# Attention scores in fp32 with two halves of the queries beside each other, and projections ahead of the loop

## The reference

```python
def _L1_gnn_ref(x, adj, node_embeddings, Wq, bq, Wk, bk, Wv):
    Q = x @ Wq + bq
    K = x @ Wk + bk
    V = x @ Wv
    score = jnp.einsum('bnc,bmc->bnm', Q, K)
    score = jax.nn.softmax(score, axis=1)
    score = jnp.einsum('bnm,mc->bnc', score, adj)
    out = jnp.einsum('bnm,bmc->bnc', score, V)
    return jax.nn.relu(out)
...
x = _layernorm(x + _L1_gnn_ref(x, adj, ...), axis=-1)
```

## Time and profile before

| | us |
|---|---|
| median of 3 runs | 790.41 (790.21 to 796.23) |
| the profiled execution | 792.9 |
| its span, first to last instruction | 790.8 |
| TensorE (PE) busy | 684.2 |
| VectorE (DVE) busy | 430.1 |
| ScalarE (ACT) busy | 340.7 |
| GpSimd (POOL) busy | 290.8 |

### The profile page before, as it was taken

The page is one execution under the profiler, slowest core; times in us unless marked ns, Lnnn a source line. Parts: engine busy times, 40 slices in busy tenths (PEclk is TensorE's granted clock), DMA queues, the critical chain, the costliest instruction groups (busy, mean ns, idle before and its releaser), DMA issues. The chain is left out here.

```text
span 790.8 us, 9801 instructions
## 1 busy us (share of the span) xinstructions
PE 684.2 (87%) x3408; PEld 474.6 (60%) x3408; DVE 430.1 (54%) x963; ACT 340.7 (43%) x649; POOL 290.8 (37%) x273
## 2 busy tenths in 40 slices
PE   6869988898898896988889847997999999999992
PEld 2767765566567682333233325886776767678882
DVE  1675747667289404656567655111566656671165
ACT  1851334444473504554645521312344646364214
POOL 0350115655448200101041483001567676750036
PEclk9988999999997998999999967999999999999996
DMA  8110030000000120303030010000000000000013
GB/s 307 54 54 2 1 107 0 1 1 1 1 2 0 24 58 1 80 2 79 1 80 1 1 57 1 1 1 0 2 1 1 1 1 0 1 2 1 1 28 80
DMA packets 14931, 20.44 MB, mean 26 GB/s; under 512 B 10064, under 2 KB 10064, under 8 KB 14880
## 3 DMA queue, kind: packets, MB, share of 16 engines
q1 hardware_dynamic: 14368, 18.16, 8.3%
q10 hardware_dynamic: 512, 1.60, 0.6%
HBM read 11.37 MB, written 2.10 MB: 17 GB/s over the span
## 5 line engine op out<-in xcount | busy, mean ns | idle before, releaser
L1879 DVE SCALAR_TENSOR_TENSOR arena<-PS,WT,arena 128x256 f32<-128x256 f32 x160 | 77.4, 484 | 67.2 <-PE PS L2003 43.1
L1551 DVE TENSOR_REDUCE arena<-PS 128x1 f32<-128x1024 f32 x64 | 75.4, 1220 | 44.2 <-PE PS L1249 44.2
L163 POOL TENSOR_TENSOR LN_Y<-LN_V,CN 128x16 f32<-128x16 f32 (+1 forms) x17 | 48.4, 2848 | 71.5 <-DVE LN_V L155 71.5
L1434 POOL TENSOR_TENSOR arena<-arena 128x128 f32<-128x128 f32 x32 | 13.0, 405 | 166.7 <-DVE arena L1557 166.7
L1795 ACT ACTIVATE spare<-PS,WT 128x256 f32<-128x256 f32 x96 | 38.9, 473 | 71.9 <-DVE arena L1879 70.3
L1395 ACT ACTIVATE arena<-PS,arena 128x1024 f32<-128x1024 f32 x44 | 48.7, 1111 | 48.7 <-DVE arena L1551 48.7
L1990 PE MATMUL PS<-WH,KH 128*128 128x512 f32 x128 | 54.3, 424 | 10.5 <-POOL KL L1701 10.0
L1243 PE MATMUL PS<-QMV,KST 128*128 128x512 f32 x128 | 44.7, 440 | 11.5 <-DVE arena L1534 5.3
L1990 PE MATMUL PS<-WH,KL 128*128 128x512 f32 x128 | 51.4, 401 | 0.0
L1990 PE MATMUL PS<-WL,KH 128*128 128x512 f32 x128 | 51.0, 398 | 0.0
L1243 PEld LDWEIGHTS PS<-QMV,KST 128*128 128x128 f32 x128 | 19.6, 188 | 45.0 <-issue 18.2
(11 more groups left out here) (285 smaller groups left out, 1620.1 us busy)
## 6 DMA issues: line engine op xcount, KB each, us to landing
arena<-in_adj_tr SPq DMA_DIRECT2D x8, 512.0 KB, 5.8
arena<-in_x_tr SPq DMA_DIRECT2D x4, 512.0 KB, 8.5
arena<-in_x_nat SPq DMA_DIRECT2D x1, 2048.0 KB, 8.8
KLO<-QMV SPq DMA_DIRECT2D x8, 256.0 KB, 3.4
QMV<-KST SPq DMA_DIRECT2D x8, 256.0 KB, 2.8
KST<-KST SPq DMA_DIRECT2D x8, 256.0 KB, 2.9
out<-arena SPq DMA_DIRECT2D x8, 256.0 KB, 3.4
arena<-in_w SPq DMA_DIRECT2D x2, 512.0 KB, 4.1
```

The lines of the kernel that those rows point to most:

```text
L163: pool.tensor_tensor(LN_Y[:, at:at + n], LN_V[:, at:at + n], CN[:, C_NEGH:C_NEGH + n], ALU.pow).then_inc(ln_rstd, 1)
L1551: dve.tensor_reduce(NMX[:, i, par:par + 1], banks("S", 2 * i + par), AX.XY, ALU.max, negate=True).then_inc(max_ready, 1)
L1879: dve.scalar_tensor_tensor(acc, PS[:, four_banks(t, j), d * F:(d + 1) * F], WT[:, e:e + 1], acc, ALU.mult, ALU.add).then_inc(acc_step, 1)
```

## The change

K and Q are kept in fp32 and not split. `project` uses one order of weights (K above Q) for both graphs of a pair; ScalarE evicts the even graph and VectorE the odd one, with bias, to KQ. DMAs bring the first 512 queries to the low half of the partitions and the last 512 to the high half (MOVED), and then put K into both halves of KQ. A score matmul has 64 rows; the two halves of one graph's queries lie beside each other in the array. Each graph's scores are signalled on their own.

All projections come before the loop: those of pairs 1 to 3 behind adjacency tiles 0 to 2, in banks 0 to 3. The adjacency tiles 6 and 7 move behind the scores of step 0, into banks 6 and 7. The residual stands ahead of the maxima of m = 4. Tensors are laid out anew.

```diff
-        KST = [[rounded(f"KST{i}{par}", at * SLOT + par * N, [P, N]) for par in range(2)] for i, at in enumerate((4, 0))]
-        QMV = [[rounded(f"QMV{i}{par}", at * SLOT + (2 * (1 - i) + par) * N, [P, N]) for par in range(2)] for i, at in enumerate((4, 2))]
-        KLO = [rounded(f"KLO{i}", 2 * SLOT + (2 + i) * N, [P, N]) for i in range(2)]
+        KQ = [[column(4, 0), column(4, 1)], [column(4, 3), spare[:, 0:N]], [column(0, 0), column(0, 1)], [column(0, 2), column(2, 3)]]
+        MOVED = [column(4, 2), spare[:, N:2 * N], column(2, 2), column(0, 3)]
...
-            if i % NT == 2 and i // NT + 1 < BP:
-                fills += [("KQ", 2 * (i // NT + 1)), ("KQ", 2 * (i // NT + 1) + 1)]
...
+        def av_bank(t):
+            return (6 if t >= NT - 2 else 4) + t % 2
...
+                low, high = slice(0, 64), slice(64, 128)
+                for q in range(BP):
+                    for par, evicted in enumerate((k_out, q_out)):
+                        b, both, halves = 2 * q + par, KQ[q][par], MOVED[q][:, par * HALF:(par + 1) * HALF]
+                        sp.wait_ge(evicted, q + 1)
+                        sp.dma_start(halves[low, :], both[high, 0:HALF]).then_inc(q_moved[b], 16)
+                        sp.dma_start(halves[high, :], both[high, HALF:N]).then_inc(q_moved[b], 16)
+                    for par in range(2):
+                        b, both = 2 * q + par, KQ[q][par]
+                        sp.wait_ge(q_moved[b], 32)
+                        sp.dma_start(both[high, :], both[low, :]).then_inc(k_moved[b], 16)
...
+                for t in range(NT - 2):
+                    adjacency_times_values(t)
+                    if t + 1 < BP:
+                        project(t + 1)
 
                 def scores(i):
                     q, m = i // NT, i % NT
-                    if m == 0:
-                        for par in range(2):
-                            pe.wait_ge(khi_moved[par], 16 * (q + 1))
                     for par in range(2):
+                        if m == 0:
+                            pe.wait_ge(k_moved[2 * q + par], 16)
                         banks_free("S", 2 * i + par)
                         for half in range(2):
-                            c = slice(half * HALF, (half + 1) * HALF)
-                            pe.matmul(banks("S", 2 * i + par)[:, half, :], KST[q % 2][par][:, tile(m)], QMV[q % 2][par][:, c],
-                                      start=True, stop=False)
-                    for half in range(2):
-                        c = slice(half * HALF, (half + 1) * HALF)
-                        for par in range(2):
-                            r = slice(64 * par, 64 * par + 64)
-                            ins = pe.matmul(banks("S", 2 * i + par)[:, half, :], KLO[q % 2][r, tile(m)], QMV[q % 2][par][r, c],
-                                            start=False, stop=True)
-                            if half == 1:
-                                ins.then_inc(s1_ready, 1)
+                            r = slice(64 * half, 64 * half + 64)
+                            ins = pe.matmul(banks("S", 2 * i + par)[:, half, :], KQ[q][par][r, tile(m)],
+                                            MOVED[q][r, par * HALF:(par + 1) * HALF], start=True, stop=True)
+                        ins.then_inc(s1_ready, 1)
...
                         scores(i)
-                        if m == 2 and q + 1 < BP:
-                            project(q + 1)
+                        if i == 0:
+                            adjacency_times_values(NT - 2)
+                            adjacency_times_values(NT - 1)
...
                 for i in range(PAIRS + 1):
                     q, m = i // NT, i % NT
                     if i < PAIRS:
+                        if m == 4 and q >= 1:
+                            residual(q - 1)
```

More of the change, by code:

```diff
@@ L57 @@
 W_BKQ = W_V + P
-W_EMB = W_BKQ + 2
+W_EMB = W_BKQ + 1
 W_L3 = W_EMB + NT * D
@@ L1058, in program @@
             sem(s) for s in ("xT1_ready", "xT1_outA", "xT1_outD", "v_ready", "v_h", "v_out", "av1_ready", "av1_outA", "av1_outD"))
-        kqb_ready, kqh_out, kql_out, s1_ready, max_ready, p_ready = (
-            sem(s) for s in ("kqb_ready", "kqh_out", "kql_out", "s1_ready", "max_ready", "p_ready"))
-        klo_moved, qhi_moved, khi_moved = ([sem(f"{s}{i}") for i in range(2)] for s in ("klo_moved", "qhi_moved", "khi_moved"))
+        k_ready, k_out, q_ready, q_out, s1_ready, max_ready, p_ready = (
+            sem(s) for s in ("k_ready", "k_out", "q_ready", "q_out", "s1_ready", "max_ready", "p_ready"))
+        q_moved = [sem(f"q_moved{b}") for b in range(2 * BP)]
+        k_moved = [sem(f"k_moved{b}") for b in range(2 * BP)]
         rz1_ready, avn_ready, pv_done, o_copied, oT_ready, o_out, centred, centredD, x2_done, x2_doneD = (
@@ L1076, in banks @@
         def banks(kind, i):
-            at = 2 * i if kind == "KQ" and i < 2 else 2 * (fills.index((kind, i)) % 3)
+            at = 2 * (fills.index((kind, i)) % 3)
             return PS[:, at:at + 2, :]
+        def av_bank(t):
+            return (6 if t >= NT - 2 else 4) + t % 2
         def turned_banks(q):
@@ L1198, in banks_free @@
                     if at < 2:
-                        pe.wait_ge(kql_out, at + 1)
+                        pe.wait_ge(q_out if at else k_out, BP)
                     elif at == 2:
-                        pe.wait_ge(av1_outA, 4)
-                        pe.wait_ge(av1_outD, 4)
+                        pe.wait_ge(av1_outA, 3)
+                        pe.wait_ge(av1_outD, 3)
                     else:
                         was, j = fills[at - 3]
-                        pe.wait_ge({"KQ": kql_out, "S": p_ready, "T": o_out}[was], j + 1)
+                        pe.wait_ge({"S": p_ready, "T": o_out}[was], j + 1)
                 def project(q):
@@ L1210, in project @@
                     else:
-                        banks_free("KQ", 2 * q)
-                        banks_free("KQ", 2 * q + 1)
+                        pe.wait_ge(k_out, q)
+                        pe.wait_ge(q_out, q)
                     for half in range(2):
-                        for par in range(2):
+                        for par, (kind, ready) in enumerate((("K", k_ready), ("Q", q_ready))):
                             r = slice(64 * par, 64 * par + 64)
-                            ins = pe.matmul(banks("KQ", 2 * q + par)[:, half, :], WT[r, W_KQ:W_KQ + P],
-                                            X1T[r, q, half * HALF:(half + 1) * HALF], start=True, stop=True)
+                            ins = pe.matmul(PS[:, 2 * par + half, :], WT[r, W_KQ:W_KQ + P], X1T[r, q, half * HALF:(half + 1) * HALF],
+                                            start=True, stop=True)
                             if half == 1:
-                                ins.then_inc(kqb_ready, 1)
+                                ins.then_inc(ready, 1)
                 turn_x1(1)
@@ L1227, in _, with adjacency_times_values @@
                     values_of(q)
-                for t in range(NT):
-                    if t >= 2:
+                def adjacency_times_values(t):
+                    if t >= NT - 2:
+                        pe.wait_ge(v_out, BP + 1)
+                    elif t >= 2:
                         pe.wait_ge(av1_outD if t % 2 else av1_outA, t // 2)
-                    adjacent(pe, rest, t, PS[:, 4 + t % 2, :], lambda m: VH[:, m, :], lambda m: VL[:, m, :],
+                    adjacent(pe, rest, t, PS[:, av_bank(t), :], lambda m: VH[:, m, :], lambda m: VL[:, m, :],
@@ L1368, in projected, with av_out @@
                 def projected(q):
[L1369 to L1374, removed]
-                projected(0)
-                for t in range(0, NT, 2):
-                    act.wait_ge(av1_ready, t + 1)
-                    act.activation(AV[:, t, :], PS[:, 4, :], ACT.Copy).then_inc(av1_outA, 1)
+                    act.wait_ge(k_ready, q + 1)
+                    act.activation(KQ[q][0], PS[:, 0:2, :].rearrange("p a c -> p (a c)"), ACT.Identity,
+                                   bias=wt(W_BKQ, 1)).then_inc(k_out, 1)
+                def av_out(t):
+                    act.wait_ge(av1_ready, t + 1)
+                    act.activation(AV[:, t, :], PS[:, av_bank(t), :], ACT.Copy).then_inc(av1_outA, 1)
+                projected(0)
+                av_out(0)
+                projected(1)
+                projected(2)
+                av_out(2)
+                projected(3)
+                av_out(4)
                 def sums_out(q):
@@ L1396, in _ @@
                                        bias=NMX[:, i, par:par + 1], accum_out=ZZ[:, i, par:par + 1]).then_inc(p_ready, 1)
-                    if m == 2 and q + 1 < BP:
-                        projected(q + 1)
+                    if i == 0:
+                        av_out(NT - 2)
                 sums_out(BP - 1)
@@ L1521, in projected, with av_out @@
                 def projected(q):
[L1522 to L1525, removed]
-                projected(0)
```

(21 more changed lines are left out.)

12 lines of the change are left out of this document (4 added, 8 removed).

## The result

The changed kernel takes 766.56 us at the median of 4 runs (762.4 to 768.46) where the kernel before took 791.58: a ratio of 0.9667 (95% interval 0.9605 to 0.9729), 25 to 26 us less. Measured a second time, on another occasion, it was 763.32 against 791.44, 0.9641 (0.961 to 0.9672). The forecast for the median was 762. The profiled execution took 762.4 with a span of 760.6 us; 762.1 was forecast for the span.

A forecast was written before the change was run, and what follows sets the result against it. A loop of waits through VectorE, ScalarE and TensorE was taken to hold quiet steps, with larger losses at pair changes. Savings of 3.3 at the start, 24.5 and 0.8 at the end, 28.7 us rounded, gave 762 us, range 757 to 766 (0.68).

The forecast's parts named there:

- Score products at 1.92, a step of 3.78: Attention loop: four paired fp32 score matmuls take 1.92 us, with 1.86 for the values; a quiet step was 4.01.
- loop of 4.00 us: Quiet attention steps before: waits through VectorE, ScalarE and TensorE set the period, 1.31 + 1.25 + 0.67 + 0.77 us.
- Start of the loop: From the first adjacency matmul at 268.67 to the first values, forecast at 310.5 instead of 313.84: 3.3 us saved.
- Adjacency tiles 6 and 7 fill idle time: Behind step 0's scores, the two moved tiles (7.26 us) fill the idle time of the first maximum and exponential.
- The 29 steps and pair changes: First values to those of step 29: 109.6 us of periods plus 3.2 for three turnings and copies; 24.5 saved.
- rival B: Pair changes keep a stall, from the residual's 1.77 us thrice or a clock fall: 764 to 769; 0.20 together with A.
- The end: Values of step 29 to the last copy of the sums, 423.3 to 429.3; 0.8 us saved.
- the 21.0 us of the old pair changes: Time of the old 29 steps beyond 29 periods of 4.01 us, forecast to fall to 3.2.
- A: Attention loop stays at 4.01 us, only pair changes gain: 6.7 us dearer, 768.5; chance 0.20 together with rival B.
- C: Paired score matmuls slow each other, 0.43 us more in each of 32 steps: 776, or 778 by the skill page; chance 0.04.
- D: Score matmuls share nothing, a step takes 5.50 us: 817, slower than before; chance 0.02.
- E: More gain, from shorter switches or later stages luckier with the clock: 753 to 757; chance 0.06.

The follow-up runs named there:

- the run on one row half: Changed kernel with both halves of the queries on the low row half, so score matmuls follow each other (timing only): 818.49 us, 1.0325 of the kernel before.
- the run with one pass: Changed kernel with K and Q kept as fp32r and scores as one product without low parts, so less precise: 743.38 us, 0.9377 of the kernel before.
- the signals coupled: Changed kernel with VectorE waiting for both graphs' scores before the first maximum: 770.02 us, 0.9714 of the kernel before.
- the run with the scores only: New score products in the old order: projections in the loop, residual behind the maxima, all adjacency tiles first: 774.15 us, 0.9766 of the kernel before.

## Why the prediction was right

By its own steps:

- **Score products at 1.92, a step of 3.78.** Right: 1.92 and 3.79. The row of L1134 was the same form, and the run on one row half shows that the sharing carries it. The Trainium skill (TensorE: Matmul & The Clock Gate, Measured speedup vs the span model) has a loss in sharing between four row tiles; two tiles here show none. A record's median is 589 ns here, as in the earlier trace rows, and also in the run where nothing is shared; and the pairs start 0.43 us apart here, as the single records do there.
- **TensorE becomes the bound.** Right, shown by the run with one pass.
- **What cut the loop of 4.00 us.** Half right. The text gave the early signal as the reason that the loop has slack. With the signals coupled the quiet step hardly changes, so the early signal isn't needed for it. What is left of the explanation is that only one graph's products lie behind a freed bank and that they end in 1.1 us; this fits the rows, but no run undoes it alone. The early signal is worth 4.9 us, nearly all of it elsewhere: at the start, at three pair changes through ScalarE's queue, and at the end.
- **Start of the loop.** 41.8 forecast, 42.57 measured. The first tile with its projection was sized well (5.79 us, 5.80 forecast). The switch between shapes was sized too small: the prediction had 0.1 for the second switch of a projection, but tiles 1 and 2 with their projections took 5.77 each instead of 5.63, and tiles 3 to 5 11.10 instead of 10.89. Tiles 6 and 7, for which it had no switch, took 7.47 instead of 7.26. The wait in step 2 came at the place forecast.
- **Adjacency tiles 6 and 7 fill idle time.** Overstated. They are worth 0.7 us, since without them TensorE waits only 0.60 us more in the first steps than with them. The sum didn't lean on it; the wording did.
- **The 29 steps and pair changes.** 112.8 forecast, 113.4 measured: the turning is 1.02, not 0.85, and the wait for the copy 0.16 to 0.23 for 0.2. The residual without a wait of TensorE: right. Undone it costs 0.92 each time in the new kernel, not the 1.77 of rival B.
- **The end.** 6.0 forecast, 5.99 measured.
- **Where the 21.0 us of the old pair changes went.** The text saved them as one term and let the moves stand for it. The products' form alone, in the old order, already takes them to 123.7 - 29 x 3.78 = 14.1. Why is only partly shown. The two projections among the 29 steps waited 1.86 us and ran 1.92 at full clock, where before it was 2.70 and about 3.6: some 5 of the 6.9 us.
- **"The other two pair changes look alike".** Misread. In the kernel before, only two of the three pair changes hold a projection; there the values lie 10.31 us apart, and the clock is down. The third holds none (no pair follows), and its 4.85 us ran at full clock. The sum isn't touched, as it took the pair changes as one measured total.

The rivals: A falls by the steps, B by the clock and the waits, C and D by the pair spacing, E has no sign. The stretch was forecast at 160.6 and measured at 162.0. That the span still came out 1.5 us under its forecast is luck: the stages outside the stretch, which the forecast took as unchanged, were 2.9 us shorter in this execution. The median of the first runs came out 4.6 us over the forecast. The four executions had spans of 760.6, 763.0, 766.6 and 766.7 at mean clocks of 0.949, 0.948, 0.943 and 0.943. Both profiled executions have the same stretch to 0.02 us, which speaks for the other stages; but where the executions without a profile lost their time stays open.

## What to carry to other kernels

When a loop is held by a chain of waits, ask how much of TensorE's work lies between the release of a buffer and the signal of its result; making that piece short can pay even if the total work grows (3.67 to 3.79 us here, while the step fell from 4.01; that the short piece did it is worked out from the rows, as no run lengthens it alone). Two fp32 matmuls on 64 rows in different row halves and different banks cost about what one costs (eight records in 1.92 us, against 3.62 in one row half), so an fp32 product can replace a split one. Price a moved piece by undoing it alone: three moves here were worth 4.2, 3.0 and 0.7 us, and the one that seemed to fill the most idle time was worth the least.

## What the runs showed of the hardware

The changed stretch, 162 us long, repeated to 0.02 us between two executions (162.01 and 162.03) and the three undone moves added up to 0.1 us, while the unchanged stages ahead of it ended between 266.4 and 271.9 us. In the latest one, the run with one pass, the stretch from 109 to 124 us, which no edit touches, was granted a clock of 0.66 (0.50 from 116.4 to 123.0) where the changed kernel had 0.89. The rows, first of the run with one pass, then of the changed kernel:

```profile
109.00:124.00 15.00, 12.78 (x42) 9.15 (x43) 7.75 (x16) 4.58 (x10) 4.35 (x4) 0.66 0.26 99
```

```profile
109.00:124.00 15.00, 13.65 (x65) 9.82 (x65) 10.77 (x23) 6.61 (x15) 5.65 (x6) 0.89 0.14 51
```

TensorE was busy for much of it in both. So part of the scatter between executions comes from time at 1.2 GHz in stages that the edit doesn't touch.

The length of a wait alone doesn't say whether the clock falls. A wait of 1.86 us ahead of a projection did not bring it down (1.00 from 330 to 342 us in the run with the scores only), and 2.70 us came ahead of 0.57 in the kernel before. But in the run with one pass, where the steps around it hold less TensorE work, a wait of 1.60 us came ahead of a fall at the last two pair changes, and at the first the same wait did not (0.84, 0.84 and 1.00 over the 10 or 11 us around them).
